# Loops written out as straight code, the queries' mask moved to VectorE, one normalisation moved between batches

## The reference

```
xn = layernorm(x)
out = x + retention_layer(xn) + local_attention_layers(xn)

local_attention_layers, 2 layers, 8 heads of 64, windows of 64 tokens:
  q, k, v = split(shift(x) @ wqkv);  q, k = rotary(l2norm(q) * qs), rotary(l2norm(k) * ks)
  x = x + softmax(mask(q @ k.T)) @ v @ wo          # keys: the own window and the one before
  x = x + (a * gelu(g)) @ w2,   a, g = split(layernorm(shift(x)) @ w1 + b1)

retention_layer, 16 heads of 8:
  q, k = l2norm(gn(x) @ qw.T), l2norm(gn(x) @ kw.T);  v = gn(x) @ vw.T
  y = ((q @ k.T) / sqrt(8) * decay(n - m)) @ v      # causal, per head
  x = x + y @ ow.T;   x = x + silu(gn(x) @ w1.T) @ w2.T
```

## Time and profile before

| | |
|---|---|
| median of three runs | 1040.29 us (1039.1 to 1043.27) |
| the profiled execution | 1042.24 us, its span 1040.4 us |
| instructions in the span | 27565 |
| granted PE clock, mean | 0.953 of full speed |
| busy share of the span | PE 85%, DVE 68%, ACT 64%, POOL 60% |

### The profile page before, as it was taken

The page is one execution under the profiler, slowest core; times in us unless marked ns, Lnnn a source line. Parts: engine busy times, 40 slices in busy tenths (PEclk is TensorE's granted clock), DMA queues, the critical chain, the costliest instruction groups (busy, mean ns, idle before and its releaser), DMA issues.

```text
span 1040.4 us, 27565 instructions
## 1 busy us (share of the span) xinstructions
PE 885.7 (85%) x10836; PEld 593.6 (57%) x10836; DVE 704.3 (68%) x1161; ACT 661.3 (64%) x1291; POOL 623.0 (60%) x491
## 2 busy tenths in 40 slices
PE   1667889889879798798898969999999999999876
PEld 1336666656646556666566645756565655656552
DVE  5865765746656557466576577869696969696833
ACT  0444757837658468376474747868686868677643
POOL 4587675855756647647566566757575756565600
PEclk9989999989999899898899989999999999999997
DMA  9000000000000000000000000000000000000000
GB/s 290 13 1 3 2 3 2 2 4 1 2 3 1 3 2 1 4 1 1 3 1 3 1 2 1 2 1 21 0 20 0 20 0 20 0 20 0 21 22 10
DMA packets 20455, 13.18 MB, mean 13 GB/s; under 512 B 4578, under 2 KB 19596, under 8 KB 20236
## 3 DMA queue, kind: packets, MB, share of 16 engines
q1 hardware_dynamic: 15108, 10.49, 3.3%
q10 hardware_dynamic: 5256, 1.31, 0.7%
HBM read 9.70 MB, written 2.10 MB: 11 GB/s over the span
## 4 chain that ended last, share of the span: by engine, by line
PE 43%; DVE 18%; ACT 10%; issue 10%; POOL 4%; DVEq 1%; ACTq 0%; POOLq 0%
DVE m L717 4%; PE pQK L1133 4%; PE pT L1006 4%; PE pM L1203 3%; PE pS L1064 3%; PE pT L1049 3%; PE pM L1081 3%; PE pQK L1296 3%; PE pS L1038 3%; PE pV L1099 3%; DVE xa L880 2%; POOL rn L360 2%; DVE ss L707 2%; DVE mx L727 2%; DVE aqk L889 1%
## 5 line engine op out<-in xcount | busy, mean ns | idle before, releaser
L360 POOL TENSOR_TENSOR rn<-rn,half_neg 128x16 f32<-128x16 f32 x64 | 187.5, 2929 | 5.3
L358 POOL TENSOR_SCALAR rn<-ss 128x16 f32<-128x16 f32 x64 | 16.3, 254 | 230.1 <-DVE ss L707 228.8
L373 POOL TENSOR_TENSOR m<-m 128x1024 f32<-128x1024 f32 x64 | 150.8, 2356 | 0.0
L1133 PE MATMUL pQK<-wqkv,hT 128*128 128x512 f32 x256 | 124.8, 611 | 3.1 <-DVE m L717 3.1
L380 POOL TENSOR_TENSOR qkn<-m,rn 128x1024 f32<-128x1024 f32 x64 | 123.7, 1933 | 6.1 <-POOL m L373 2.0
L727 DVE TENSOR_REDUCE mx<-pS 128x8 f32<-128x1024 f32 x64 | 78.1, 1220 | 63.7 <-PE pS L1038 63.6
L516 ACT ACTIVATE kT<-pT 128x512 f32<-128x512 f32 x64 | 38.0, 594 | 112.9 <-PE pT L1006 112.6
L1006 PE MATMUL pT<-cst,qkn 128*128 128x128 f32 x512 | 73.5, 290 | 23.1 <-issue 19.1
L556 ACT ACTIVATE sq<-pQK 128x1024 f32<-128x1024 f32 x64 | 65.4, 1022 | 27.8 <-PE pQK L1133 27.6
L707 DVE TENSOR_REDUCE ss<-sq 128x16 f32<-128x1024 f32 x64 | 77.5, 1211 | 7.6 <-ACT sq L556 7.6
L540 ACT ACTIVATE prT<-pT 128x1024 f32<-128x1024 f32 x64 | 65.0, 1016 | 23.7 <-PE pT L1049 23.5
(11 more groups left out here) (168 smaller groups left out, 2077.9 us busy)
## 6 DMA issues: line engine op xcount, KB each, us to landing
x<-in_L_attn_x SPq DMA_DIRECT2D x4, 512.0 KB, 9.1
xs<-in_L_attn_x SPq DMA_DIRECT2D x8, 256.0 KB, 2.8
out<-aqkT SPq DMA_DIRECT2D x8, 256.0 KB, 2.2
wqkv<-in_L_ffn_wqkv SPq DMA_DIRECT2D x2, 768.0 KB, 9.7
tab<-in_k_tab SPq DMA_DIRECT2D x1, 1024.0 KB, 10.3
w<-in_L_ffn_w SPq DMA_DIRECT2D x2, 341.0 KB, 10.3
wo<-in_L_ffn_wo SPq DMA_DIRECT2D x2, 256.0 KB
cst<-in_k_cst ACTq DMA_DIRECT2D x1, 404.5 KB, 3.9
```

The source lines that it names most:

```text
L360: eng.tensor_tensor(rn[:, k % 2, :], rn[:, k % 2, :], half_neg[:, 0:2 * H], ALU.pow).then_inc(S["rn_done"], 1)
L373: eng.tensor_tensor(m1[:, k % 2, :], m1[:, k % 2, :], m2[:, k % 2, :], ALU.add).then_inc(S["add_done"], 1)
L1133: mm = eng.matmul(pQK[:, g * 512:(g + 1) * 512], hT[:, k, :], wqkv[:, l, g * 512:(g + 1) * 512], start=True, stop=True)
```

## The change

1. `run_bodies` writes all steps out: Python loops take the place of the two hardware loops, on PE, DVE, ACT and POOL. SP keeps its loop. Waits that compared with a register become waits on constants.
2. PE transposes keys into `pM` and queries into `pT[:, 128:256]`, each with its own semaphore. Ahead of the queries' transpose it waits for the batch before's `vx`, since `vx` is read from the same bank. ScalarE copies the keys alone to `akT`, which lies in `osb`, now with memory of its own. VectorE masks the queries straight out of PSUM (`dve_group_queries`), ahead of all its other work on the batch, and PE waits for that before it writes the values of the block into `pT`. GpSimd masks the keys alone.
3. In `pool_retention` the last batch's `pool_norm` stands behind the masks of batch 1, its `pool_add` behind those of batch 2; `pool_scale` stays at the end.

```diff
             body((0, 1), (0, 0), None)
-            with eng.Fori(2, NT) as t:
+            for t in range(2, NT):
                 body((0, t), (0, t - 1), (0, t - 2))
...
             for b in range(NB):
-                pool_mask_qk(eng, t, b)
+                pool_mask_keys(eng, t, b)
                 if b == 0:
                     pool_retention_norm(eng, t, 1)
                 if b + 2 < NB:
                     pool_retention_norm(eng, t, b + 2)
+                if b == 1:
+                    pool_norm(eng, n, last)
+                if b == 2:
+                    pool_add(eng, n, last)
             if old:
                 pool_ln(eng, old)
-            pool_norm(eng, n, last)
-            pool_add(eng, n, last)
             pool_scale(eng, n, last)
...
-                need(eng, A["qx"], n - 1)
-                eng.activation(aqkT[:, k % 2, :, :], pM[:, 0:256].rearrange("p (g n) -> p g n", g=2),
-                               ACT.Copy).then_inc(A["t_ev"], 1)
+                need(eng, A["kx"], n - 1)
+                eng.activation(akT[:, k % 2, :], pM[:, 0:P], ACT.Copy).then_inc(A["t_ev"], 1)
...
+        def dve_group_queries(eng, t, b):
+
+            n = 4 * t + b
+            shape = [P, NBL, NG, BL]
+            eng.wait_ge(A["q_mm"], n + 1)
+            need(eng, A["y_mm"], n - 1)
+            eng.tensor_tensor(qx[:, b % 2, :, :, :],
+                              pT[:, P:2 * P].rearrange("p (c n) -> p c n", c=NBL).unsqueeze(2).broadcast_to(shape),
+                              group_mask.unsqueeze(1).unsqueeze(3).broadcast_to(shape), ALU.mult).then_inc(A["qx"], 1)
...
             for k in range(NB + 1):
+                if k < NB:
+                    dve_group_queries(eng, t, k)
                 if k > 0:
                     dve_block_scores(eng, t, k - 1)
...
-                    for g in range(2):
-                        mm = eng.transpose(pM[:, g * P:(g + 1) * P], aqk[:, k % 2, g, :], ident)
-                    mm.then_inc(A["t_mm"], 1)
+                    eng.transpose(pM[:, 0:P], aqk[:, k % 2, 1, :], ident).then_inc(A["t_mm"], 1)
+                    need(eng, A["vx"], n)
+                    eng.transpose(pT[:, P:2 * P], aqk[:, k % 2, 0, :], ident).then_inc(A["q_mm"], 1)
...
             need(eng, A["vx"], 4 * t + b)
+            eng.wait_ge(A["qx"], 4 * t + b + 1)
             for c_ in range(NBL):
```

More of the change, by code:

```diff
@@ L194, in program @@
         avm = sb("avm", [P, 2, NBL, P])
-        aqkT = sb("aqkT", [P, 2, 2, P])
+        osb = sb("osb", [P, NB, D])
+        akT = osb[:, 0:2, :]
         araw = pr[:, :, :, :].rearrange("p u h n -> p (u h) n")[:, 0:8, :]
@@ L209, in program @@
         xs = sb("xs", [P, NB, D])
-        osb = aqkT[:, :, :, :].rearrange("p u g n -> p (u g) n")
         pQK = ctx.enter_context(nc.psum_tensor("pQK", [P, 1024], F32))
@@ L245, in program @@
         A = {n: sem(f"a_{n}") for n in (
-            "xa", "qkv_mm", "sqq", "v", "floor", "rs", "qk", "t_mm", "t_ev", "vx_mm", "vx", "kx", "qx", "st_mm", "sm",
+            "xa", "qkv_mm", "sqq", "v", "q_mm", "floor", "rs", "qk", "t_mm", "t_ev", "vx_mm", "vx", "kx", "qx", "st_mm", "sm",
             "kv_mm", "kvm", "y_mm", "yt", "faded", "state", "ow_mm", "x1", "cs")}
@@ L415, in pool_state, with pool_mask_keys @@
             eng.tensor_tensor(state[:, :, :], state[:, :, :], before[:, :, NBL - 1, :], ALU.add).then_inc(A["state"], 1)
-        def pool_mask_qk(eng, t, b):
+        def pool_mask_keys(eng, t, b):
             n = 4 * t + b
@@ L423, in pool_mask_qk @@
             eng.tensor_tensor(kx[:, b % 2, :, :, :],
-                              aqkT[:, b % 2, 1, :].rearrange("p (c n) -> p c n", c=NBL).unsqueeze(2).broadcast_to(shape),
+                              akT[:, b % 2, :].rearrange("p (c n) -> p c n", c=NBL).unsqueeze(2).broadcast_to(shape),
                               place_mask.unsqueeze(1).unsqueeze(3).broadcast_to(shape), ALU.mult).then_inc(A["kx"], 1)
[L426 to L429, removed]
         def pool_group_norm(eng, k):
```

## The result

The changed kernel takes 1034.99 us (median of 5 runs, 1034.32 to 1037.18), the kernel before in the same comparison 1041.63 (5 runs, 1039.1 to 1043.27). The ratio is 0.9945 with a 95% interval of 0.9924 to 0.9966: 6.6 us faster at the medians, 5.7 by the ratio, 3.5 to 7.9 by its interval. The profiled execution took 1036.91 us around a span of 1034.8; the one of before 1042.24 around 1040.4.

A forecast was written before the change was run, and what follows sets the result against it. Bounds: PE's five costly layer 0 jumps, otherwise a pipeline in which PE, VectorE and GpSimd take turns. Jumps -27.4 and retentions +24.6 make -2.8: 1040.29 - 2.8 = 1037.5 us, range 1026 to 1047.

The forecast's parts named there:

- The jumps, -27.4: PE's five costly loop jumps in layer 0: the stretches over them, 59.94 us together, would fall to 32.5.
- The step that chose 6.5 for a straight stretch: From a retention's last product to ScalarE's copy in the next body: straight code took 6.40 and 6.58 us, taken as 6.5.
- Waits on registers, 0: Register waits turned into constants in the written-out loops: counted 0, from two straight stretches of 6.40 and 6.58 us.
- Layer 1's jumps: PE's five jumps in layer 1's loop, 0.2 us each: counted 0, with bounds of 0 and 1.2 us.
- The mask, 1.28 later: Retention: VectorE's queries' mask, 0.68 us (upper bound 1.04), delays batch 0's `vx` and all of batch 1 by 1.28 us.
- The norm between the batches: Retention: GpSimd's norm and addition delay key masks 2 and 3; each retention takes 22.7 us, 24.6 more over eight.
- within 0.5%: Whole kernel no different from before, 1035.1 to 1045.5 us: chance 0.48, against 0.32 for faster and 0.20 for slower.
- (a): PE keeps its full clock in the written-out retentions: about 21.4 us each, total 1027; chance 0.17.
- (b): PE falls to the lower clock a second time, in the retention's tail: 1.7 us per retention, total 1051; chance 0.16.
- (c): Instructions arrive late in layer 1's written-out bodies, at most about two stalls each: 8 us, total 1045.5; chance 0.07.
- (d): PE's layer 0 jumps cost only 0.06 us, the rest a fetch straight code needs too: total 1064.6; chance 0.03.

The follow-up runs named there:

- the body without a jump: A body inside an iteration, in the kernel before with layer 1's loop made two iterations of three bodies each; that kernel measured 1045.0 us, ratio 1.0057.
- the best kernel: Against the kernel with only its loops written out, VectorE's scaling of batch 1's queries and keys put ahead of batch 0's `vx` and masked sums: 1001.77 us.

## Why the prediction was right in its way and off in size

**The jumps, -27.4: right, 1.9 too small.** The five stretches lost 29.3 us. The gap was PE's alone (the kernel with PE alone written out: 1011.0 us), and the straight code that takes its place has no stall of that kind. The step that chose 6.5 for a straight stretch took the mean of two in which the other engines still had registers in their waits, on one side or the other; with none left it takes 6.08.

**Waits on registers, 0: wrong.** This is the term of the sum that failed. Layer 1's jumps, also 0, came out of the same bodies. I reasoned from two straight stretches, of which the shorter led into the looped body. Both had something of the loop beside them, and the other looped bodies kept their registers in both, so the comparison could not show what registers cost. Measured: 0.43 us less in each of six bodies of layer 1 (2.6, over twice the upper bound of 1.2 that I had given for layer 1's jumps), 0.29 in each of six pieces of layer 0 between copy and retention (1.7), and 0.8 in the two straight stretches. In layer 1 the body without a jump at 50.40 us shows that it is not the jumps; in layer 0 the kernel with PE alone written out, at 38.53, shows that it is not on PE. Which engine's waits they are is open. Together with the 1.9 above this is 7.0 us of gain that the sum lacked.

**The mask, 1.28 later: right.** Batch 1 started 6.82 to 7.05 us into the retention (205.47 - 199.97 + 1.28 = 6.78 forecast); VectorE's mask took 0.68 to 0.69 us, the lower of my two bounds. The 0.06 us between the mask and PE's values had no row behind it and was 0.15 in step 2 (213.59 to 213.74), so the delay came out nearer 1.4. That the later batches' masks cost nothing is not shown: without the norm some 5.5 us stayed with them. `ars` of batch 3 was done 12.2 to 12.6 us into the retention, for 12.41 forecast.

**The norm between the batches: right.** Key mask 2 started at 15.4 to 15.9 us (15.66 forecast), key mask 3 at 18.7 to 19.2 (19.12), the retention ended at 22.3 to 23.5 (22.7), and the sum rose by 26.0 for 24.6. The lower clock came in all eight, as expected. The pauses in the midst of equal products, which I had seen in the straight retention of step 1, did not grow: 3.5 us over the eight, before 5.7. By themselves the two edits cost 21 and 34 us over the loops, together 26. The forecast came near because it followed one queue with both in it, and did not add two prices.

**The rest, +2.8.** The first retention starts 1.4 us later, and layer 1's ends take 1.4 more. The start varies from 76.2 to 79.1 us over the kernels here, the last body with what follows it from 61.5 to 63.4, with no tie to an edit; I have no cause for either.

The sum: -2.8 forecast, less 7.0 for registers and stretches, plus 1.4 in the retentions and 2.8 in the rest, gives the -5.6 of the two traces. The medians stand 6.6 apart. That the total came within 3 us is in part luck: 7.0 us of gain that the sum lacked met 4.2 us of loss that it lacked too, of which 2.8 have no cause that I know. The likeliest case, "within 0.5%", was missed by a hair: 0.55%, with an interval from 0.34 to 0.76.

**The rivals.** (a) Full clock in the retentions: it was below 1.00 on average in all eight. (b) A second fall in the tail: not in this kernel, but in the one with the norm and without the mask; my argument against it, that PE has work in more than half of that stretch, is not tested as the reason. (c) Late instructions in layer 1: its bodies became shorter, though the written-out code is fetched there and the loop was not. (d) Jumps worth nothing: against it stand 32 us. The rule of about 108 ns for a compare-and-branch, from the Trainium skill's "Advanced Engine Details and Errata", section Control Flow Timing, would have led there; on PE the trace differs, by the length of the code. Nor does VectorE's 0.05 to 0.07 us meet that figure, as my prediction had it: it is about half.

## What to carry to other kernels

Look for the dear jump in the loop line's own rows, engine by engine, and compare it with a straight passage over the same work: a loop whose body PE can't hold costs it 3.5 to 3.8 us at each jump and 4.6 to 6.1 with the slow clock behind it, one that it can hold 0.2 us, and only PE's need be written out to win nearly all. When two edits put work into the same engine's queue, walk that queue once with both in it, since their prices by themselves don't add: here 21 and 34 made 26. And when a change as a whole moves little, run its parts: of this one the loops alone gained 32 us, the rest gave back most of it, and the best kernel moved an instruction of VectorE the other way.

## What the runs showed that I had not expected

- A body of layer 1 takes 50.40 us with its counter in registers even where nothing jumps, and 49.97 with constants.
- The same instructions of a retention took from 17.5 to 20.9 us within one kernel (PE alone written out). The granted clock fell in six of the eight, for a shorter or longer time, after the same idleness of 3.14 us, and the pauses in the midst of equal products were between none and 1.6 us; what decides either in code that doesn't change is open. It is several times what layer 1's jumps or registers are worth, and the reason why a gain of 2.6 us could be seen in windows and not in medians.
- An idleness of PE before batch 1 that is 0.6 us shorter (2.52 for 3.14) makes 8 x 0.61 = 4.9 us by its length. At the medians the kernel with it is 7.4 us faster than the one with the loops alone. The retentions differ by 12.5 us in these two traces, but only by 6.3 from the trace with layer 0 alone written out, whose layer 0 is the same as that of the loops alone: how much of the difference is the clock and how much the spread of it from run to run is not settled.
- Straight code isn't free of idleness without a releaser either: where small products follow one another closely, PE pauses in their midst, 1.85 us in the row shown above. What it waits for there is not shown.
